# Graph attention on one core: a 64-column clear on GpSimd behind every second gather

## What is computed

```
score = K[src] * Q[dst] / sqrt(dh) * (edge_attr @ WE)
score = exp(clip(score.sum(-1), -5, 5))         # 8 heads of 16
wV = segment_sum(V[src] * score, dst);  Z = segment_sum(score, dst)
h = x + wV / (Z + 1e-6)
y = batchnorm(h) * gamma + beta                 # over the nodes
out = layernorm(x + y)                          # over the features
```

## Time and profile before

| | |
|---|---|
| median of 3 runs | 2586.85 us (2584.51 to 2589.57) |
| the profiled execution | 2589.74 us |
| its span, first to last instruction | 2587.5 us |
| mean granted TensorE clock | 0.644 of full speed |
| TensorE, VectorE, GpSimd busy | 79%, 63%, 62% of the span |
| gathers from the table | 1613, mean 948 ns |
| DMA | 451.67 MB, mean 175 GB/s |

### The profile page before, as it was taken

One profiled execution on the slowest core, in us unless ns is written; L12 is line 12 of the kernel. 1 busy time (PEld: TensorE's weight loads), 2 busy tenths in 40 slices (PEclk: granted clock), 3 DMA queues, 4 the chain that ended last, 5 costly groups with the idle time before them and its releaser, 6 DMA issues.

```text
span 2587.5 us, 43308 instructions
## 1 busy us (share of the span) xinstructions
PE 2047.7 (79%) x12797; PEld 1851.5 (72%) x12797; DVE 1641.1 (63%) x3734; ACT 809.5 (31%) x1876; POOL 1611.7 (62%) x1698
## 2 busy tenths in 40 slices
PE   7688878777788788887888878878877777777887
PEld 7577777667677777776777767767766767777776
DVE  5475666666666666566566665666666666666687
ACT  2342323323223223233233232323332332332335
POOL 6566666666666666666666666666666666666624
PEclk9785665666656665566566675565566665656578
DMA  9655555555555555555555555555555555555554
GB/s 340 228 164 165 171 172 176 159 178 167 161 176 177 164 165 175 181 164 161 168 182 171 164 172 168 165 168 175 176 156 181 169 156 181 169 168 166 172 198 113
DMA packets 190769, 451.67 MB, mean 175 GB/s; under 512 B 91455, under 2 KB 98959, under 8 KB 176657
## 3 DMA queue, kind: packets, MB, share of 16 engines
q1 hardware_dynamic: 111648, 235.56, 27.7%
q0 software_dynamic: 78960, 214.67, 27.5%
HBM read 420.10 MB, written 29.98 MB: 174 GB/s over the span
## 4 chain that ended last, share of the span: by engine, by line
PE 52%; issue 18%; DVE 18%; another core or an unknown queue 9%; DVEq 2%; ACT 1%; POOL 0%; DMA 0%; SPq 0%; POOLq 0%; ACTq 0%
PE eh_ps L886 19%; PE agg_ps L892 15%; PE agg_ps L894 6%; PE qe_ps L876 6%; DVE kq L1232 4%; DVE ssum L1235 4%; DVE kq L1227 3%; DVE ring L1081 2%; DVEq L1160 2%; PE aux_ps L769 1%; PE aux_ps L902 1%; DVE onehot L1156 1%; DVE acc L1170 1%; PE eh_ps L781 1%
## 5 line engine op out<-in xcount | busy, mean ns | idle before, releaser
L566 POOL DMA_INDIRECT ring<-kv_rows,src_t x1613 | 1529.0, 948 | 874.9 <-issue 413.7
L886 PE MATMUL eh_ps<-we_sb,ea 128*128 128x128 f32 x3322 | 800.3, 401 | 187.2 <-issue 165.7
L886 PEld LDWEIGHTS eh_ps<-we_sb,ea 128*128 128x128 f32 x3322 | 671.3, 292 | 247.3 <-issue 195.0
L892 PE MATMUL agg_ps<-onehot,ring 128*128 128x42 f32 x3322 | 673.2, 362 | 133.0 <-issue 132.6
L892 PEld LDWEIGHTS agg_ps<-onehot,ring 128*128 128x128 f32 x3322 | 649.7, 282 | 149.3 <-issue 148.7
L1227 DVE TENSOR_TENSOR kq<-ring,qe_ps 128x512 f32<-128x512 f32 x416 | 282.5, 679 | 577.3 <-remote 392.1
L650 ACT ACTIVATE qe_ps<-sclip 128x32 f32<-128x32 f32 x416 | 83.7, 201 | 1567.9 <-DVE sclip L1237 1019.8
L876 PE MATMUL qe_ps<-q_win,ohT 126*128 126x128 bf16 x1661 | 253.2, 289 | 104.1 <-issue 87.8
L894 PE MATMUL agg_ps<-onehot,score 128*8 128x42 f32 x3322 | 278.0, 246 | 52.3 <-issue 51.7
L644 ACT ACTIVATE ohT<-ohT,ones 126x512 bf16<-126x512 bf16 x416 | 300.1, 722 | 13.5
L876 PEld LDWEIGHTS qe_ps<-q_win,ohT 126*128 126x128 bf16 x1661 | 183.5, 135 | 164.7 <-issue 143.0
(11 more groups left out here) (163 smaller groups left out, 870.4 us busy)
## 6 DMA issues: line engine op xcount, KB each, us to landing
ea<-in_edgeT SPq DMA_DIRECT2D x104, 1024.0 KB
rel_wide<-rel_rows SPq DMA_DIRECT2D x104, 512.0 KB
ring<-kv_rows,src_t POOLq DMA_INDIRECT x1613
q_win<-q_rows SPq DMA_DIRECT2D x416, 31.5 KB
kv_rows<-ring SPq DMA_DIRECT2D x24, 512.0 KB
q_rows<-q_st SPq DMA_DIRECT2D x27, 360.0 KB
ring<-in_xT SPq DMA_DIRECT2D x12, 512.0 KB, 7.1
xs<-in_xT SPq DMA_DIRECT2D x25, 240.0 KB
```

Of the source, the lines that this page charges most:

```text
L566: pool.indirect_dma_start(out=kv[:, s, j, :], out_offset=None, in_=kv_rows, in_offset=bass.IndirectOffsetOnAxis(ap=src_t[:, n * TILES + j: ...
L886: pe.matmul(eh_ps[s % 2][:, j * P:(j + 1) * P], ea[:, s % EARS, j * P:(j + 1) * P], we_sb[:, :], start=True, stop=True)
L892: pe.matmul(msg_ps[s % 2], kv[:, room_of(s), j, D:KV], onehot[:, s % 8, j, :], start=(j == 0), stop=(j == tiles_of(n) - 1))
```

## The change

Behind the second and the fourth gather of a group (`j % 2`) GpSimd clears a new buffer `pause` of 128 partitions by 64 columns of float32, which nothing reads. Each clear counts up the semaphore `paused`, and each but the first waits until the one before it was counted. The clear behind the second gather stands inside the group; the one behind the fourth stands ahead of the next group's first gather, which waits for `agg_ready`.

```diff
+        pause = sb("pause", [P, 64])
...
+        paused = sem("paused")
...
                         out=kv[:, s, j, :], out_offset=None, in_=kv_rows,
                         in_offset=bass.IndirectOffsetOnAxis(ap=src_t[:, n * TILES + j:n * TILES + j + 1], axis=0),
                     ).then_inc(kv_landed[s], 16)
+                    if j % 2:
+                        k = (n - LIFT) * (TILES // 2) + j // 2
+                        if k:
+                            pool.wait_ge(paused, k)
+                        nc.gpsimd.memset(pause[:, :], 0.0).then_inc(paused, 1)
```

## The result

The median of 16 runs is 2590.65 us (2589.3 to 2596.09), against 2586.76 us (2584.4 to 2590.4) in 16 runs of the kernel before. The ratio is 1.002, 95% interval 1.0013 to 1.0027. That is some 4 to 5 us: the interval leaves out 1, but the difference stays within the 5 us that the prediction called no change. 2587 us was predicted. The profiled execution took 2590.26 us around a span of 2588.1.

The account below looks back on a forecast made before the run. Each gather was taken to hold TensorE back, some 1.48 us a gather, above GpSimd's 1.25. The 144 us of clears would hide in 367 us of GpSimd's waiting: 2586.85 + 0, about 2587 us, range 2475 to 2700.

Parts of the forecast that it names:

- Each gather holds TensorE's progress back by a fixed amount: Gather loop: time is the count of gathers times some 1.48 us, with GpSimd's own 1.25 us a gather below it.
- The argument from the earlier trace: Turns of 16 groups took 94.2 to 95.1 us though TensorE's matmuls and clock varied, so TensorE doesn't set the period.
- Price of a clear: GpSimd, behind second and fourth gathers: near enough 0.18 us for each of 806 clears, bounds 0 to 0.62 us.
- fits in the gap: Lower end for a clear on GpSimd: it costs nothing if it fits in the 0.30 us gap between gathers.
- the announced picture of pairs 1.43 us apart: GpSimd's timeline if right: gathers of a pair 1.25 us apart, pairs about 1.43 us apart.
- The wait for the last clear: GpSimd's wait for the clear before, finished 2.5 us earlier: costs nothing if GpSimd's own count arrives at once.
- Sum: GpSimd's group becomes 5.37 us, below 5.935; 144 us of clears come out of 367 us of waiting: change 0.
- the cover: GpSimd's slack in a group, which hides the clears: 0.92 us before, 0.56 us left; gone at 0.46 us a clear.
- TensorE's "issue" gaps: TensorE's standstills during gathers with nothing to wait for, 0.75 to 1.20 us each: unchanged in sum.
- Spacing adds: Slower rival: time behind a run of gathers is fixed, so clears lengthen each period: 2659 or 2731 us; both forms 0.30.
- Its second form: Slower rival: GpSimd is full, 1.48 us of work a gather, each clear adds: 144 us, 2731; both forms 0.30.
- Pauses let TensorE through: Faster rival: pauses every second gather keep a backlog below TensorE's stall; 112 us less, 2475, at most 2361; chance 0.25.

Follow-up runs that it names:

- third set: The changed kernel with its 64-column clears run again on another chip beside the kernel before: 2620.87 us against 2617.54, ratio 1.0017.
- clear900: The changed kernel with clears of 900 columns instead of 64, against the kernel before on the same chip: 2747.32 us, ratio 1.0476.

## Why the prediction was right, and where it wasn't

- **What bounds the kernel.** "Each gather holds TensorE's progress back by a fixed amount" stood in the main. Half the bytes, clears of 400 columns and the edge products done twice leave the time within 1.4%, one gather more or less moves it by 20 to 21%. Of the size, 1.48 us is right as a mean over four; the increment is 1.31 to 1.38 with a constant of 0.5 to 0.8 us a group. What is held was left open and is now narrower: TensorE's signals. That this holds only on some chips wasn't foreseen; that the change was timed on one of them is luck, since on the other kind GpSimd has no slack to give. The argument from the earlier trace rows was weaker than it read: fewer matmuls at a lower clock made TensorE's busy time 79.3, 77.1 and 78.5 us a turn, nearly as steady as the turns, so the windows didn't rule TensorE out. Three and five gathers did.
- **Price of a clear.** The term was mis-sized: 0.18 us predicted, 0.03 measured. The busy time was right (0.16 against 0.167), the gap behind it wasn't. I had kept the full 0.30 us gap and added 0.03, and it shrinks to 0.16. So this is the lower bound of the text, "fits in the gap", nearly reached, and the announced picture of pairs 1.43 us apart didn't arise (1.27). That GpSimd's waits would fall by 140 us was wrong with it. They fell from 446.0 in 262 waits to 395.5 in 243 + 22 = 265 (both without the wait of the opening, 12.0 and 11.3). A part of the fall is only the gap of 0.30 or 0.16 that stands inside each; less the gaps, 367 became 395.5 - 265 x 0.16 = 353, so 14 us went to clears where 399 x 2 x 0.03 = 24 were to be found.
- **The wait for the last clear** costs nothing, as argued: the clears had 0.4 us of idle time ahead of them in all.
- **Sum.** Change 0 was forecast, and +0.20% was measured on the first chip and +0.17% in the third set. With the true price the cover is 0.87 us a group instead of 0.56, so the sum stands more safely than it was argued. The point at which it breaks was put at 0.46 us a clear. 0.31 us was hidden and 0.865 + 0.16 - 0.30 = 0.73 wasn't, where a group of 6.45 us is 5.01 + 2 x 0.72.
- **TensorE's "issue" gaps**, forecast unchanged: 418.7 us (149.5 + 110.9 + 115.1 + 43.2) against 437.8.
- **The rivals.** "Spacing adds" is refuted by the 400 columns: 247 us of clears, 6 us in the time. What was said for it, that no run restarts sooner than the wait shown, was a misreading: in the kernel before runs of four restart after 0.49 to 2.04 us (median 1.27) and runs of eight after 2.01 to 2.29. Its second form, hidden work behind each gather, was tied to the Trainium skill's page Perfetto Trace Analysis (DMA Instruction, SWDGE), by which the engine's program for a gather ends later than its profiled end. Here a clear begins at the profiled end in all 806 cases, and with 900 columns the visible pieces fill the period to 0.01 us, so no hidden work of any size is left; on this point the trace decides. "Pauses let TensorE through" had something real in it: clear900 does free TensorE's signals. But the spacing at which they are free lies above the 1.48 us that the hold-back itself costs, so GpSimd's own pace is the bound by then.

**What stays open.** The 0.2% itself. The ratios of 64 and 400 columns overlap (1.0017 and 1.002 against 1.0022 and 1.003), but not because length costs nothing: the longer clears cost 10 to 13 us in the loop and give back 7 in the opening. Where the 4 us of the 64 columns come from nothing here isolates. Then what holds the signals back, whether it goes by gathers or by rows, and why one chip of those used doesn't have it. And the change on such a chip, which didn't come up again: there GpSimd's pace is the bound and 24 us of clears should show, an estimate of +1.1%. A version without the wait on `paused` wasn't tried. None of the kernels that compute the whole was faster than the kernel before.

## What to carry to other kernels

When no engine is full, look for what repeats equally in stretches that otherwise differ, and test it by its count: one instance more, one less. An instruction put into a gap may take the place of the gap, so read distances from start to start, not busy times. And before an effect is put down to the program, run the same kernel on more than one chip: here the bound itself changed.

## What was unexpected of the hardware

- The same kernel took 2587, 2622 and 2618 us in three sets and 2162 in a fourth, 16% less, with steady runs in each (2157.64 to 2165.07 in the fourth). In the three a further gather costs 1.31 to 1.38 us (measured in one of them) and TensorE's signals come late; in the fourth a gather costs GpSimd's 1.25 and signals come in 0.01 us.
- An indirect gather holds GpSimd for 0.95 us with 128 rows, of 1 KB or of 512 B, and for 0.90 with 64 rows. The gap to the next gather is 0.30 us, and 0.16 behind a memset.
- Memsets of 128 partitions took 0.167 us (64 columns), 0.448 (400) and 0.865 (900), 0.0008 us a column.
- TensorE's granted clock went from 0.64 to 0.81 of full speed (between its levels of 1.2 and 2.4 GHz) when the edge products were done twice, and was 0.59 with the 900-column clears. On the chip without waits it went from 0.71 to 0.58 when matmuls were left out. These are means over the whole kernel.
